# Taking out the constant products that TensorE makes between stages of a one-core fusion block

## What is computed

```python
# 1. tokens of the image at three patch sizes; the coarser two are interpolated to 256 tokens
outs = [level(x, idx0, W0, b0), interp(level(x, idx1, W1, b1)), interp(level(x, idx2, W2, b2))]
h = concat([concat(outs, -1) @ Wf.T + bf, txt], axis=1)
# 2. a selective state-space block (causal convolution of 4 taps, 16 states for each channel)
x_branch, z = split(layernorm(h) @ in_proj_w.T)
u = silu(conv(x_branch) + conv_b)
dt = softplus(u @ dt_w.T + dt_b);  Bv = u @ B_w.T;  Cv = u @ C_w.T
state = exp(dt * A) * state + dt * Bv * u        # scanned over the 384 tokens
y = (sum_s(state * Cv) + D * u) * silu(z)
h = h + layernorm(y @ out_w.T + layernorm(h)) * ln_g + ln_b
# 3. a mixture of 8 experts, 2 for each token
top2 = top_k(layernorm(h) @ Wr.T, 2)
h = h + sum_k softmax(top2)[k] * (gelu(xn @ Wi[e_k].T + bi[e_k]) @ Wo[e_k].T + bo[e_k])
```

## Time and profile before

| | us |
|---|---|
| median of 3 runs | 541.25 (520.53 to 545.41) |
| the profiled execution | 521.7 |
| its span, first to last instruction | 519.9 |
| mean granted clock of TensorE over the span | 0.924 |

### The profile page before, as it was taken

One profiled execution on the slowest core, in us unless ns is written; L12 is line 12 of the kernel. 1 busy time (PEld: TensorE's weight loads), 2 busy tenths in 40 slices (PEclk: granted clock), 3 DMA queues, 4 the chain that ended last, 5 costly groups with the idle time before them and its releaser, 6 DMA issues.

```text
span 519.9 us, 7212 instructions
## 1 busy us (share of the span) xinstructions
PE 438.6 (84%) x2381; PEld 309.7 (60%) x2381; DVE 294.1 (57%) x497; ACT 206.9 (40%) x422; POOL 215.0 (41%) x169
## 2 busy tenths in 40 slices
PE   5787979999798867778778998699999999999920
PEld 4345636456543323334334687588999999999910
DVE  4400365374799999999992873814434344443232
ACT  1312183375465646654650132103444444444400
POOL 6777303000166656664661000423444444444232
PEclk9977998999989999998999997758999999999975
DMA  8110005800000000000004021001111111112053
GB/s 220 26 6 5 5 1 208 339 0 1 0 1 0 0 0 0 0 2 0 0 0 153 30 81 42 0 16 44 54 48 53 53 47 49 46 52 53 24 179 109
DMA packets 14817, 25.32 MB, mean 49 GB/s; under 512 B 4989, under 2 KB 11886, under 8 KB 13774
## 3 DMA queue, kind: packets, MB, share of 16 engines
q1 hardware_dynamic: 10446, 17.37, 9.7%
q0 software_dynamic: 4352, 7.71, 5.7%
HBM read 19.26 MB, written 5.80 MB: 48 GB/s over the span
## 4 chain that ended last, share of the span: by engine, by line
PE 53%; issue 21%; DVE 12%; POOL 5%; ACT 4%; DMA 3%; DVEq 1%; SPq 0%; POOLq 0%; ACTq 0%
PE ps L858 12%; PE ps L841 8%; DVE ps L1287 7%; PE ps L673 5%; PE ps L847 5%; PE ps L647 3%; PE ps L646 3%; DVE w_all L1296 3%; PE ps L817 2%; DVE state L1296 2%; POOL w_all L507 2%; PE ps L831 1%; PE ps L615 1%; PE ps L616 1%; POOL h_tok L550 1%
## 5 line engine op out<-in xcount | busy, mean ns | idle before, releaser
L507 POOL TENSOR_TENSOR hc<-state,x_cm 128x768 f32<-128x768 f32 x24 | 43.6, 1815 | 74.3 <-DVE state L1296 74.3
L1048 ACT ACTIVATE decay<-dt_cm,a_neg 128x766 f32<-128x766 f32 x48 | 44.8, 936 | 57.5 <-DVE state L1296 30.6
L543 POOL DMA_INDIRECT y_dram<-u_cm,tok_out x31 | 35.3, 1139 | 75.1 <-ACT u_cm L1135 73.0
L673 PE MATMUL ps<-cst 128*128 128x256 f32 x208 | 55.2, 428 | 6.8 <-DMA cst<-in_cst 5.5
L673 PEld LDWEIGHTS ps<-cst 128*128 128x128 f32 x208 | 44.4, 218 | 15.8 <-DMA cst<-in_cst 5.5
L507 POOL TENSOR_TENSOR w_all<-w_all,x_cm 128x768 f32<-128x768 f32 x24 | 43.6, 1817 | 22.7 <-DVE w_all L1296 22.7
L484 POOL DMA_INDIRECT w_all<-in_pix,gidx x42 | 43.2, 1030 | 14.7 <-issue 12.5
L1120 ACT ACTIVATE u_cm<-ps,x_cm 128x128 f32<-128x128 f32 x96 | 26.6, 377 | 55.2 <-PE ps L847 55.2
L1287 DVE TENSOR_TENSOR ps<-dtu_cm,ps 128x768 f32<-128x768 f32 x48 | 45.3, 944 | 4.0 <-PE ps L708 3.9
L719 PE MATMUL ps<-c_parts,pick 128*128 128x384 bf16 x96 | 24.9, 342 | 23.3 <-ACT x_cm L1056 23.3
L1296 DVE TENSOR_TENSOR_SCAN state<-decay,ps 128x768 f32<-128x768 f32 x24 | 42.1, 1754 | 2.7
(11 more groups left out here) (215 smaller groups left out, 750.8 us busy)
## 6 DMA issues: line engine op xcount, KB each, us to landing
w_all<-in_w_all SPq DMA_DIRECT2D x8, 1156.0 KB, 8.6
w_all<-y_dram SPq DMA_DIRECT2D x3, 768.0 KB, 6.5
x_dram<-dt_cm SPq DMA_DIRECT2D x3, 384.0 KB, 2.6
out<-h_tok SPq DMA_DIRECT2D x3, 384.0 KB, 2.6
w_all<-in_pix,gidx POOLq DMA_INDIRECT x42, 2.4
w_all<-in_i SPq DMA_DIRECT2D x2, 256.0 KB
dt_cm<-x_dram,tok_in POOLq DMA_INDIRECT x31, 2.8
y_dram<-u_cm,tok_out POOLq DMA_INDIRECT x31, 2.5
```

The source lines that it names most:

```text
L507: nc.gpsimd.tensor_tensor(hcs[p], states[p], c_sb[p], ALU.mult).then_inc(hc_rdy, 1)
L543: pool.indirect_dma_start(y_dram, bass.IndirectOffsetOnAxis(ap=tok_out[:, i:i + 1].bitcast(U32), axis=0), y_out[:, i % 2, :], None).then_i ...
L673: nc.tensor.matmul(ps[:, bank, 0:256], ident, cst[:, 0:256], start=True, stop=True)
L1048: nc.scalar.activation(decay[:, p, :, 1:L], unit(dt3, US[n], 1, L - 1), ACT.Exp, scale=a_neg[:, g, bass.ds(s, 1)]).then_inc(decay_rdy, 1)
```

## The change

The table, the helper and its ten calls are taken out. All other instructions, on every engine, stand in the same order with the same waits; TensorE's list is 104 products (208 records) shorter.

```diff
-        WARM = {"input weights": 10, "interpolated levels": 8, "fine tokens": 3, "last convolution": 10,
-                "last steps": 24, "router's rows": 32, "later rows": 3, "last rows": 2, "slots": 8, "first tile": 4}
...
-            def keep_warm(n, bank):
-                for _ in range(n):
-                    nc.tensor.matmul(ps[:, bank, 0:256], ident, cst[:, 0:256], start=True, stop=True)
             pe.wait_ge(ld_cst, 16)
-            keep_warm(WARM["input weights"], 0)
             pe.wait_ge(ld_in, 16 * N_IN)
             in_projection(0)
...
             pe.wait_ge(ev_tok, V_UP)
-            keep_warm(WARM["interpolated levels"], 0)
             tokens_from_patches(0)
...
             in_projection(1)
-            keep_warm(WARM["fine tokens"], 0)
             tokens_from_patches(1)
...
             gate_projection(2)
-            keep_warm(WARM["last convolution"], 0)
             scan_inputs(2)
-            keep_warm(WARM["last steps"], 0)
...
-            keep_warm(WARM["router's rows"], 7)
...
             router_transposes(0)
-            keep_warm(WARM["later rows"], 1)
             router_transposes(1)
             router_logits(0)
-            keep_warm(WARM["last rows"], 1)
             router_transposes(2)
...
-            keep_warm(WARM["slots"], 0)
             pe.wait_ge(gt_rdy, 1)
...
-            keep_warm(WARM["first tile"], 2)
```

## The result

| | before, us | after, us |
|---|---|---|
| median of 5 runs beside each other | 520.89 (520.53 to 545.41) | 565.78 (549.30 to 568.22) |
| the profiled execution | 521.7 | 568.22 |
| its span | 519.9 | 566.4 |
| ratio after to before | | 1.054 (1.052 to 1.057) |

The change makes the kernel slower. Each program's executions fall into two groups: two of the five of before lie at 541 and 545 and three at 521, three of the five of after at 566 to 568 and two at 549, and the ratio compares the lower groups, 549 with 521. So the median of 565.78 is set by three of five executions that took the upper value. The profile shown is of one of these; one at the lower value is shown with the experiments.

The account below looks back on a forecast made before the run. TensorE was taken to bound the front and the experts, VectorE the scan. Front +41.8, scan +0.5, router +2.5 and first tile +0.7 sum to +45.5 on 521.7, 567, lowered to 566 us for uncertain prices; range 533 to 575.

Parts of the forecast that it names:

- case A: Whole front: without the products TensorE's clock stays low up to the scan; +45.5 us in all, 566 us; chance 0.48.
- Rival B: Second image block: its fusion raises the clock again, so only the loss ahead stays; +28.5 us, 550 us; chance 0.28.
- steps 1 to 8: Front from the first block to the first half of scan_inputs(2), priced at the low clock: shift reaching +44.4 us.
- The price of scan_inputs: Front: the 64 records of a scan_inputs call take 8.3 us more at the low clock, ends 0 and +11.75.
- The 512-column price: Projections of the front: each 512-column record takes 0.45 us more at the low clock, ends nothing and 0.53.
- The coarse levels, +2.9: Coarse levels at the low clock: 12 transposes +1.3 us and 40 small records +1.6, bringing the shift to +9.4.
- The first step, +41.8: Scan: its first step begins 41.8 us later, after 2.6 us gained from the products ahead of it.
- The second half of scan_inputs(2) is covered: Ahead of the scan: this half's +4.2 us cost nothing, since softplus and split take 13.6 us.
- The rest: Behind the scan's start: first steps +0.5 us, router +2.5, L817 0, first expert tile +0.7.
- steps 1 to 5: Front from the first block through the second image block; in Rival B they stand at +23.5 us.
- Rival C: Front: real work such as the first block's in projection raises the clock by itself; 529 us; chance 0.13.
- Rival D: Whole kernel: the clock doesn't depend on the products, so only their 12.2 us are gained; 509.5 us; chance 0.06.

Follow-up runs that it names:

- changed_again: The changed kernel run once more with no edit, on a chip where before takes 520.85 us: 549.26 us, ratio 1.054.
- half_rows: The kernel before with all ten groups of constant products, each product using 64 rows instead of 128: 576.23 us, one execution, where before has a median of 553.13.
- before_again: The kernel before run once more with no edit, for its trace on the chip of changed_again: 520.26 us.
- one_recovery: The changed kernel plus four constant products between the second image block's fusion and its gate projection: 550.22 us, ratio 1.057.
- back_only: The kernel before without the five product groups of the front, the five behind the scan kept: 567.36 us, one execution, against 553.1.
- fitted_more: the fitted version with 11 instead of 6 products ahead of the first image block's transposes: 502.95 us, ratio 0.966.
- front_only: The kernel before without the five product groups behind the scan, the five of the front kept: median 557.81 us, ratio 1.006.
- the fitted version: The kernel before with its products refitted to the places where TensorE waits: 536.70 us on one chip, 505.25 on another, ratio 0.970 on both.

## Why the prediction held, step by step

Predicted 566.0 us (533 to 575); the median is 565.78 and the profiled execution 568.22. Its second case, 550, is the time of the other executions, 549. The agreement of the median to 0.2 us is luck. The kernel has two values, and of its ten executions on record (the five of the median, a sixth of 548.11 us and the four of changed_again) three took the upper one and seven the lower; a median of changed_again alone is 549.26. The prediction gave A 0.48 and B 0.28, from one trace and the spread of three times; the ten lean the other way. What held is the mechanism and both sums, not the choice between them.

| place (line before) | predicted shift, us | case A measured: before, after, shift |
|---|---|---|
| coarse levels begin (L562) | +6.5 | 25.29, 31.71, +6.4 |
| first L592 | +5.0 | 46.76, 52.82, +6.1 |
| scan_inputs(0) begins | +8.9 | 52.60, 62.53, +9.9 |
| its 64 records | +8.3 | 11.75, 20.14, +8.4 |
| second L592 | +21.7 | 72.41, 95.29, +22.9 |
| scan_inputs(1) begins | +26 | 86.72, 113.39, +26.7 |
| scan_inputs(2) begins | +40.2 | 114.20, 155.51, +41.3 |
| its first half | +4.2 | 6.17, 10.88, +4.7 |
| first step of the scan (L708) | +41.8 | 136.69, 180.57, +43.9 |
| router's rows (L778) | -3.1 on the shift of the scan | 307.71, 348.04, +40.3 |
| logits done (L802) | +44.8 | 323.66, 369.47, +45.8 |
| end of the span | +45.5 | 519.9, 566.4, +46.5 |

- **The clock stays low without the products (steps 1 to 8): right for this execution.** Every record of the front has the low length. The reading behind it, that alternating 128 and 64 rows didn't raise it, is borne out: of the 150 us of busy time in the front (0 to 180 us) most is such records, and half_rows shows it for 64 rows alone.
- **The price of scan_inputs, +8.3 with no low row to read it from: right,** +8.4, 0.131 a record, where half of the +0.235 of 256 columns is 0.118.
- **The 512-column price, 0.45 a record: right,** 0.47, which is also what twice 0.235 gives (L629 begins at 13.82, L630 at 15.83, so 1.00 a record).
- **The coarse levels, +2.9: mis-sized by a little.** The 40 small records were put at +1.6 with ends at 0 and 3.1; they cost +2.5 (L577 and L573 took 3.57 us, now 6.04). This miss and a few tenths at the small waits give the 1 us that runs through the table.
- **The first step, +41.8: 2.1 short.** 1.1 was there already, 0.5 is the size of the first half, and 0.5 is TensorE's start behind the last cast: I had counted the 2.6 us of products from the cast, but L694 starts 0.48 us after it (180.57 against 180.09).
- **The second half of scan_inputs(2) is covered: right.** TensorE then waits 4.09 us for VectorE's last part.
- **The rest: right.** The router's rows regain 3.6 us (3.1 predicted), the low logits give it back (0.26 a record from the first), L799 takes 5.35 as L817 did.
- **Rival B was no rival but the second value,** and the more frequent one. The same instructions give 549 where the second fusion raises the clock and 566 where it doesn't. (Its +23.5 for steps 1 to 5 is 23.0 by the steps themselves; the first VectorE step is 25.9 later than in before_again, +24.8 predicted.)
- **Rival C, real work raises the clock by itself: fell as a forecast of the time, not as a fact.** In the first block L632 and L633 stream without a gap for 4 us, and the records are low. But real work did raise it from cold elsewhere: the twelve transposes of the coarse levels in three of the seven traces that reached them at the low clock (half_rows, one_recovery, back_only), and the second fusion with the projection behind it. The first of these was gone again before L580 and saved 2.3 us where it saved anything. So "the low clock for the whole front" was too strong. The sentence of the Trainium skill ("TensorE: Matmul & The Clock Gate", section "What's actually happening") that activity releases the throttle agrees with the full products and with those of 64 columns (twenty records in 6.3 and 6.2 us). It doesn't agree with the twenty records of 64 rows, which stayed low for 8.9 us.
- **Rival D, 509.5, the gain without the loss: fell,** though the gain is real. fitted_more, which keeps the clock for most of the front and saves most of the delays, reaches 503.

## What to carry to other kernels

Work that looks useless may be holding a clock: before products like these are taken out, price the front at the low clock from any stretch of the trace that ran low, record by record, since busy time alone doesn't tell which level it will run at. Look at how many rows the matmuls use, not only at how dense they are. Then put the products into the waits, up to their ends and as little beyond as can be; that was worth 3.4% over the kernel before, and taking them all out cost 5.4% at the lower of its two values and 8.6% at the upper.

## What the runs showed of the hardware

- Records of 64 rows, alone or in turn with 128, did not raise TensorE's clock from 1.2 GHz (20 of them in 8.9 us and twice 16 in 7.19 us in half_rows; the projections of the changed kernel). Records of 128 rows and 64 columns did. A high clock stayed high through products of 64 rows (63 of them in 13.76 us).
- The same instructions may or may not raise it. The sixteen 192-column records of the second fusion (128 and 65 rows in turn), with the 512-column projection behind, raised it from low in seven of ten traces, in changed_again within 3.4 us, and not in the profile after, in front_only and in half_columns. The same sixteen in the first image block, with `scan_inputs(0)` behind, ran low in six traces and never raised it. What decides is open.
- On two of four chips the coarse levels stood still up to 64 us; before took 32 us more there (553 against 521), and the fitted version too (537 against 505). GpSimd's last gather had just been issued. The cause is open.
- Ahead of the first recorded change of level, the view of the granted clock shows 1.00, whatever the clock is. The length of a known record is the safer witness.
